# A graph attention layer: the mish ratio in the products' PSUM bank, and gathers that wait for the products 14 groups back

## The chip, the core and the metric

One core of a Trainium2 chip runs the kernel. The metric is the device time of one execution in microseconds (us); shorter is better. The engines are TensorE (PE, its weight loads PEld), VectorE (DVE), ScalarE (ACT), GpSimd (POOL) and SyncE (SP, which issues most of the plain DMAs). Each runs its own instructions strictly in order; semaphores tie them together.

## What is computed

A graph of 6250 nodes (128 features, 4 heads of 32) and 206250 edges, sorted by receiver. The reference, cut to what matters:

```python
e_att  = nodes[senders] @ Ws + Ws_b + edges @ We + We_b      # per edge, 4 heads x 32
recv   = nodes[receivers] @ Wr + Wr_b
logits = einsum(mish(e_att + recv), attn_w) + attn_b         # mish(x) = x * tanh(softplus(x))
w      = exp(logits - segment_max(logits, receivers))
w      = w / segment_sum(w, receivers)[receivers]
x      = layernorm(x + segment_sum(w * e_att, receivers))
```

## The kernel before

**Tables first.** A prologue computes two tables, `xs_table` (nodes times Ws, with biases) and `xr_table` (nodes times Wr), on PE (L754) and DVE (L1042), and stores them to HBM.

**Windows and groups.** The edges are then worked off in 51 windows of 4096 edges (128 partitions by 32 columns). A window has 8 groups (`NG`) of 4 columns, numbered g = 0 to 7; there are 408 groups. With `at(w, g) = w * 8 + g + 1` the groups are counted through, and every semaphore of a per-group step is compared with such a count.

**One group** goes through these steps, each one instruction on 128x512 numbers unless a count is given:

- POOL gathers the 4 columns of sender rows, `gathers`, L717, 4 indirect DMAs, into the buffer `gath` in SBUF (named `landing` in the profile). Two windows fit, so a buffer is used again 16 groups later.
- DVE makes the one-hot matrices of the receivers, `one_hots`, L1113. PE transposes edges and one-hots, `turn`, L793 and L798; ACT copies both out of PSUM, L907 and L914.
- PE multiplies, `products`, L815 and L816, 16 matrix instructions, into one of two banks, `ps_z[g % 2]`.
- DVE adds the gathered rows, `add_gathered`, L1122, from `ps_z` into `Z` in SBUF; its semaphore is `z_ready`.
- ACT computes the mish ratio in `tbuf` (SBUF) in five instructions, L923 to L939; the last one gives `ratio_ready`.
- DVE forms mish (L1129, semaphore `mish_ready`), the scores (L1138) and their sums per head (L1144).
- A window later, when the maxima of the segments are known, DVE scales `Z` (`messages`, L1205) and PE sums it per receiver (`sums`, L827, 8 matrix instructions per group).

**The order is written by hand.** Each engine has a function `window` that goes through g = 0 to 7 (below, "step g" of an engine). What a step holds:

- PE, step g: `products(g)`, `turn` of the group two ahead, then old sums: in steps 0 to 3 the groups 4 to 7 of two windows ago, in steps 5, 6, 7 the groups 0, then 1, then 2 and 3 of the window before.
- ACT, step g: the two copies of the group two ahead, then the five ratio instructions of group g.
- DVE, step g: `one_hots` of the group three ahead, `add_gathered(g)`, messages (none in step 3, two in step 4, else one), then `mish`, `score` and `reduce_heads` of group g - 1. Small instructions of the softmax and the layer norm (`aside`) stand between them in steps 3 to 6.

The one-hot buffer holds two windows, so `one_hots` waits until the sum of the group 16 earlier has been taken (`sum_ready`). In DVE's steps 5, 6 and 7 that sum stands at the end of PE's step of the same number; in steps 0 to 4 it stands in PE's step before. `products(g)` waits for the copies of its own group and for the add of group g - 2, which read its bank. POOL's gathers of a group wait for the products `AHEAD` groups back.

Of the kernel before, what the change touches and what calls it, by code (L numbers as in the profile page):

```python
# [21 lines left out]
ACT = mybir.ActivationFunctionType  # L22
# [3 lines left out]
D = 128  # L26
# [11 lines left out]
TINY = 1e-30  # L38
EPS = 1e-5
PREP = 6  # L40
AHEAD = 4
SEG_A, SEG_B, SEG_C = 3, 3, 5
ENDS_READ = 2
SEG = SEG_A + SEG_B + SEG_C
# [23 lines left out]
def gat_kernel(nc, x, src, dst, edges, ws_k, ws_b, wr_k, wr_b, we_k, we_b, attn_w, attn_b, out):  # L68
# [14 lines left out]
    with ctx:  # L83
        def sb(name, shape, dt=F32):
            return ctx.enter_context(nc.sbuf_tensor(name, shape, dt))

        def sem(name):
            return ctx.enter_context(nc.semaphore(name))
# [14 lines left out]
        Zv = Z[:, :, :].rearrange("p b (t c) -> p b t c", c=ZC)  # L103
# [52 lines left out]
        c_ln2 = sb("c_ln2", [P, 1])  # L156
# [32 lines left out]
        def ps(name, shape):  # L189
            return ctx.enter_context(nc.psum_tensor(name, shape, F32))  # L190
# [3 lines left out]
        ps_z = [ps(f"ps_z{i}", [P, GT, D]) for i in range(2)]  # L194
# [68 lines left out]
        z_ready = sem("z_ready")  # L263
# [4 lines left out]
        ratio_ready = sem("ratio_ready")  # L268
        mish_ready = sem("mish_ready")
# [17 lines left out]
        def at(w, g):  # L287

            return w * NG + g + 1

        def wait(eng, s, value):

            if not isinstance(value, int) or value > 0:
                eng.wait_ge(s, value)

        def wait_apart(eng, s, value, past):


            eng.wait_ge(s, value)
            eng.sem_inc(past, 1)  # L300

        def there(w):

            return not isinstance(w, int) or 0 <= w < W
# [398 lines left out]
        def _(pool):  # L703
# [7 lines left out]
            def gathers(w, b):  # L711

                for g, (a, n) in enumerate(GROUPS):
                    if not isinstance(w, int) or at(w, g) > AHEAD:
                        wait_apart(pool, z_ps, at(w, g) - AHEAD, past_pool)
                    for t in range(a, a + n):
# [22 lines left out]
        def _(pe):  # L739
# [62 lines left out]
            def products(w, b, k, g):  # L802

                a, n = GROUPS[g]
                q = g % 2
                pe.wait_ge(edgeT_ready, at(w, g))
                pe.wait_ge(onehotT_ready, at(w, g))
                wait(pe, z_ready, at(w, g) - 2)
                if g == 0:
                    if not there(w - 1):  # L810
                        pe.wait_ge(s_first_xr, 1)
                    else:
                        pe.wait_ge(xr_landed[b], k * 16 + (16 if b else 0))
                for j in range(n):
                    nc.tensor.matmul(ps_z[q][:, j, :], edgeT[:, q, j, :], we_sb[:, :], start=True, stop=False)  # L815
                    mm = nc.tensor.matmul(ps_z[q][:, j, :], onehotT[:, q, j, :], xr_buf[:, b, :],  # L816
                                          start=False, stop=True)
                mm.then_inc(z_ps, 1)
# [56 lines left out]
        def _(act):  # L875
# [50 lines left out]
            def ratio_step(w, g, k):  # L926
                tb = tbuf[:, g % NT, 0:GROUPS[g][1] * D]
                if k == 0:
                    act.wait_ge(bounded, at(w, g))
                    nc.scalar.activation(tb, tb, ACT.Exp, bias=c_zmax[:, 0:1], scale=-1.0).then_inc(exp_done, 1)  # L930
                elif k == 1:
                    act.wait_ge(exp_done, at(w, g))
                    nc.scalar.activation(tb, tb, ACT.Square, bias=c_one[:, 0:1]).then_inc(sq_done, 1)  # L933
                elif k == 2:
                    act.wait_ge(sq_done, at(w, g))
                    nc.scalar.activation(tb, tb, ACT.Ln, bias=c_one[:, 0:1]).then_inc(ln_done, 1)  # L936
                else:
                    act.wait_ge(ln_done, at(w, g))
                    nc.scalar.activation(tb, tb, ACT.Exp, bias=c_ln2[:, 0:1], scale=-1.0).then_inc(ratio_ready, 1)  # L939

            def items(w):
                act.wait_ge(ends_ps, w + 1)
# [47 lines left out]
        def _(dve):  # L990
# [45 lines left out]
            for done in range(2 * NB):  # L1036
                a, n = BATCHES[done % NB]
                stage, bias = (xs_stage, bias_s) if done < NB else (xr_stage, bias_r)
# [86 lines left out]
            def mish(w, b, g):  # L1125
                a, n = GROUPS[g]
                dve.wait_ge(ratio_ready, at(w, g))
                tb = tbuf[:, g % NT, 0:n * D].rearrange("p (t d) -> p t d", d=D)
                nc.vector.scalar_tensor_tensor(out=tb, in0=tb, scalar=1.0, in1=Zv[:, b, a:a + n, 0:D],  # L1129
                                               op0=ALU.subtract, op1=ALU.mult, reverse0=True)\  # L1130
                    .then_inc(mish_ready, 1)

# [214 lines left out]
```

## Time and profile before

| | |
|---|---|
| Three runs | 2601.63, 2613.3, 2615.81 us; median 2613.3 us |
| Profiled execution, from its first to its last instruction (span) | 2661.8 us |
| Busy: PE, DVE, ACT, POOL | 1917.4, 1895.0, 1927.7, 1575.1 us |
| Mean granted TensorE clock | 0.835 of full speed |
| Bytes over HBM | 240.18 MB, 90 GB/s on average |

The span of the profiled execution is 48.5 us (1.9%) above the median of the runs, though it leaves out what lies before its first and after its last instruction. No separate time of that execution is listed beside its span. Busy times are averages over steps with different limits: an engine at 72% can be the one that all wait for in one step and idle in the next. "remote" in a row means that the wait ended by a semaphore update that the profile does not pin to an instruction that ended just before it; "issue" means that no wait is seen.

### The profile page before, as it was taken

The page shows a single profiled execution, that of the slowest core. Times are in us where ns is not written, and L with a number is a line of the kernel's source. Part 1 is how long each engine was busy: PE and PEld are TensorE (multiplying, and loading weights), DVE is VectorE, ACT ScalarE, POOL GpSimd, SP SyncE. Part 2 cuts the span into 40 slices and gives each one's busy share as a digit, 9 for nine tenths or more (in the row PEclk, how much of TensorE's full clock was granted, in tenths as well). Part 3 has the DMA queues.
Part 4 walks back from the last instruction along what each step waited for, and adds up shares of the span by engine and source line. Part 5 has one row for each costly group of instructions (what it writes and reads, how often), then busy time and mean ns, then how long its engine had stood idle before and what let it go on. Part 6 is the DMA issues. An engine that isn't in the chain of part 4 may idle for free.

```text
span 2661.8 us, 45397 instructions
## 1 busy us (share of the span) xinstructions
PE 1917.4 (72%) x13621; PEld 1789.2 (67%) x13621; DVE 1895.0 (71%) x3941; ACT 1927.7 (72%) x3126; POOL 1575.1 (59%) x1640
## 2 busy tenths in 40 slices
PE   5667777777776777776776777776777777776776
PEld 5567666766666776766666766666667676666665
DVE  2676777777777767776676777766777777677766
ACT  1777777777777777777777777777777777777774
POOL 2666656656666665666566656656666666556661
PEclk8888888888888887888888888878888888878877
DMA  6422322322232322232232232232223232223220
GB/s 191 130 77 80 105 83 78 112 79 77 81 111 77 97 96 77 77 113 79 76 112 79 78 105 86 78 100 90 78 93 99 79 98 95 77 86 104 79 79 17
DMA packets 106714, 240.18 MB, mean 90 GB/s; under 512 B 45800, under 2 KB 72546, under 8 KB 99658
## 3 DMA queue, kind: packets, MB, share of 16 engines
q1 hardware_dynamic: 53334, 132.54, 14.6%
q0 software_dynamic: 52224, 107.06, 14.1%
q10 hardware_dynamic: 1128, 0.25, 0.0%
q8 instruction: 13, 0.21, 0.0%
q14 instruction: 15, 0.12, 0.0%
HBM read 229.98 MB, written 9.74 MB: 90 GB/s over the span
## 4 chain that ended last, share of the span: by engine, by line
DVE 36%; PE 20%; another core or an unknown queue 18%; issue 17%; ACT 7%; DVEq 1%; DMA 1%; ACTq 0%; SPq 0%
PE ps_sum L827 7%; DVE Z L1122 6%; DVE tbuf L1138 6%; DVE tbuf L1129 6%; DVE Z L1205 5%; PE ps_z L815 4%; PE ps_z L816 4%; DVE onehot L1113 4%; DVE logit L1144 2%; PE ps_edgeT L793 2%; ACT tbuf L933 1%; ACT tbuf L930 1%; ACT tbuf L936 1%; ACT tbuf L923 1%
## 5 line engine op out<-in xcount | busy, mean ns | idle before, releaser
L717 POOL DMA_INDIRECT landing<-xs_table,src_i x1632 | 1574.2, 965 | 1034.1 <-issue 448.3
L815 PE MATMUL ps_z<-we_sb,edgeT 128*128 128x128 f32 x3264 | 767.2, 320 | 83.3 <-issue 82.4
L816 PE MATMUL ps_z<-xr_buf,onehotT 128*128 128x128 f32 x3264 | 751.9, 315 | 72.3 <-issue 71.5
L827 PE MATMUL ps_sum<-Z,onehot 128*128 128x132 f32 x3264 | 558.9, 321 | 204.7 <-DVE att L1224 95.2
L815 PEld LDWEIGHTS ps_z<-we_sb,edgeT 128*128 128x128 f32 x3264 | 613.0, 232 | 100.9 <-issue 97.3
L816 PEld LDWEIGHTS ps_z<-xr_buf,onehotT 128*128 128x128 f32 x3264 | 609.4, 231 | 83.1 <-issue 82.8
L827 PEld LDWEIGHTS ps_sum<-Z,onehot 128*128 128x128 f32 x3264 | 485.6, 224 | 223.8 <-issue 149.4
L1113 DVE TENSOR_TENSOR onehot<-iota_f,ps_dve 128x512 f32<-128x512 f32 x408 | 276.0, 677 | 432.5 <-remote 352.6
L923 ACT ACTIVATE tbuf<-Z,c_zmax 128x512 f32<-128x512 f32 x408 | 296.2, 726 | 165.7 <-DVE Z L1122 85.9
L907 ACT COPY edgeT<-ps_edgeT 128x512 f32<-128x512 f32 x408 | 235.3, 577 | 229.4 <-remote 179.9
L798 PE MATMUL ps_onehotT<-ident_half,onehot 128*128 128x128 bf16 x1632 | 176.6, 232 | 241.8 <-issue 103.8
L1122 DVE TENSOR_TENSOR Z<-ps_z,landing 128x512 f32<-128x512 f32 x408 | 278.5, 683 | 88.6 <-remote 72.9
L914 ACT CAST onehotT<-ps_onehotT 128x512 f32<-128x512 bf16 x408 | 238.8, 585 | 132.9 <-remote 120.5
L798 PEld LDWEIGHTS ps_onehotT<-ident_half,onehot 128*128 128x128 bf16 x1632 | 125.0, 104 | 291.3 <-issue 226.7
L930 ACT ACTIVATE tbuf<-tbuf,c_zmax 128x512 f32<-128x512 f32 x408 | 294.7, 722 | 13.3
L793 PE MATMUL ps_edgeT<-ident,landing 128*128 128x128 f32 x1632 | 281.1, 295 | 32.3 <-issue 31.9
L933 ACT ACTIVATE tbuf<-tbuf,c_one 128x512 f32<-128x512 f32 x408 | 294.6, 722 | 13.3
L936 ACT ACTIVATE tbuf<-tbuf,c_one 128x512 f32<-128x512 f32 x408 | 294.5, 722 | 13.3
L939 ACT ACTIVATE tbuf<-tbuf,c_ln 128x512 f32<-128x512 f32 x408 | 294.0, 721 | 11.6
L1129 DVE SCALAR_TENSOR_TENSOR tbuf<-tbuf,Z 128x512 f32<-128x512 f32 x408 | 279.3, 685 | 26.6 <-ACT tbuf L939 21.2
L1138 DVE TENSOR_TENSOR tbuf<-tbuf,ps_dve 128x512 f32<-128x512 f32 x408 | 278.4, 682 | 9.0
L1144 DVE TENSOR_REDUCE logit<-tbuf 128x16 f32<-128x512 f32 x408 | 277.9, 681 | 7.3
(110 smaller groups left out, 1228.3 us busy)
## 6 DMA issues: line engine op xcount, KB each, us to landing
landing<-in_edge_attr_dram SPq DMA_DIRECT2D x51, 2048.0 KB
landing<-xs_table,src_i POOLq DMA_INDIRECT x1632
x_in<-in_x_dram SPq DMA_DIRECT2D x51, 64.0 KB
xr_in<-xr_table SPq DMA_DIRECT2D x51, 64.0 KB
out_dram<-y_out SPq DMA_DIRECT2D x51, 64.0 KB
xr_buf<-xr_table SPq DMA_DIRECT2D x50, 64.0 KB
xs_table<-onehot SPq DMA_DIRECT2D x2, 896.0 KB
xr_table<-landing SPq DMA_DIRECT2D x1, 1568.0 KB
```

The source lines that it names most:

```text
L717: nc.gpsimd.indirect_dma_start(gath[b][:, t, :], None, xs_dram, bass.IndirectOffsetOnAxis(ap=src_i[:, b, t:t + 1], axis=0))\
L793: tr = nc.tensor.transpose(ps_edgeT[g % 2][:, j, :], edge_buf[:, b, a + j, :], ident[:, :])
L815: nc.tensor.matmul(ps_z[q][:, j, :], edgeT[:, q, j, :], we_sb[:, :], start=True, stop=False)
L816: mm = nc.tensor.matmul(ps_z[q][:, j, :], onehotT[:, q, j, :], xr_buf[:, b, :], start=False, stop=True)
L827: mm = nc.tensor.matmul(ps_sum[:, 0:ZC], OHv[:, b, t, :], Zv[:, b, t, :], start=(t == 0), stop=(t == T - 1))
L923: nc.scalar.activation(tb, Zv[:, b, a:a + n, 0:D], ACT.Relu, bias=c_zmax[:, 0:1], scale=-1.0)\
L930: nc.scalar.activation(tb, tb, ACT.Exp, bias=c_zmax[:, 0:1], scale=-1.0).then_inc(exp_done, 1)
L1113: nc.vector.tensor_tensor(OHv[:, b, a:a + n, :], iota_f[:, :].unsqueeze(1).to_broadcast([P, n, P]), local[:, b, a:a + n].unsqueeze(2).to_b ...
L1122: nc.vector.tensor_tensor(Zv[:, b, a:a + n, 0:D], ps_z[g % 2][:, 0:n, :], gath[b][:, a:a + n, :], ALU.add).then_inc(z_ready, 1)
L1129: nc.vector.scalar_tensor_tensor(out=tb, in0=tb, scalar=1.0, in1=Zv[:, b, a:a + n, 0:D], op0=ALU.subtract, op1=ALU.mult, reverse0=True)\
L1138: nc.vector.tensor_tensor(tb, tb, row.to_broadcast([P, n, D]), ALU.mult).then_inc(scored, 1)
L1144: nc.vector.tensor_reduce(logit[:, b, :, a:a + n].rearrange("p h t -> p t h"), tb, AX.X, ALU.add)\
```

## The change

Three things change. ACT's last ratio instruction writes to the bank `ps_z[g % 2]`, which the group's own products had filled and the add has read, instead of to `tbuf`. DVE's mish instruction takes the ratio from there, so it reads one operand from PSUM and one from SBUF instead of two from SBUF; its output is still `tbuf`. Since the bank is now in use for longer, `products(g)` waits for `mish` of group g - 2 instead of for its add. Apart from that, `AHEAD` goes from 4 to 14. A group's products wait for mish, hence for the add, of two groups earlier, so products 14 back still imply the add 16 back that has freed the gather buffer.

```diff
-AHEAD = 4
+AHEAD = 14
...
                 pe.wait_ge(edgeT_ready, at(w, g))
                 pe.wait_ge(onehotT_ready, at(w, g))
-                wait(pe, z_ready, at(w, g) - 2)
+                wait(pe, mish_ready, at(w, g) - 2)
...
                     act.wait_ge(ln_done, at(w, g))
-                    nc.scalar.activation(tb, tb, ACT.Exp, bias=c_ln2[:, 0:1], scale=-1.0).then_inc(ratio_ready, 1)
+                    nc.scalar.activation(ps_z[g % 2][:, :, :].rearrange("p t d -> p (t d)"), tb, ACT.Exp,
+                                         bias=c_ln2[:, 0:1], scale=-1.0).then_inc(ratio_ready, 1)
...
                 dve.wait_ge(ratio_ready, at(w, g))
                 tb = tbuf[:, g % NT, 0:n * D].rearrange("p (t d) -> p t d", d=D)
-                nc.vector.scalar_tensor_tensor(out=tb, in0=tb, scalar=1.0, in1=Zv[:, b, a:a + n, 0:D],
+                nc.vector.scalar_tensor_tensor(out=tb, in0=ps_z[g % 2][:, :, :], scalar=1.0, in1=Zv[:, b, a:a + n, 0:D],
                                                op0=ALU.subtract, op1=ALU.mult, reverse0=True)\
                     .then_inc(mish_ready, 1)
```

No instruction of PE, DVE or ACT changes its place; on POOL waits fall away ahead of the first groups. On PE the place that matters is a step of the window loop: the wait of the products now names `mish_ready`, and behind it, in the same in-order queue, stand the transposes of the group two ahead and a sum. After the change a piece of the loop reads:

```order
L815 MATMUL ps_z<-we_sb,edgeT 128x128 [waits mish_ready,onehotT_ready,edgeT_ready]
L816 MATMUL ps_z<-xr_buf,onehotT 128x128
L815 MATMUL ps_z<-we_sb,edgeT 128x128
L816 MATMUL ps_z<-xr_buf,onehotT 128x128
L815 MATMUL ps_z<-we_sb,edgeT 128x128
L816 MATMUL ps_z<-xr_buf,onehotT 128x128
L815 MATMUL ps_z<-we_sb,edgeT 128x128
L816 MATMUL ps_z<-xr_buf,onehotT 128x128
L793 MATMUL ps_edgeT<-ident,landing 128x128 [waits edgeT_ready]
L793 MATMUL ps_edgeT<-ident,landing 128x128 x3
L798 MATMUL ps_onehotT<-ident_half,onehot 128x128 [waits onehotT_ready,onehot_ready]
L798 MATMUL ps_onehotT<-ident_half,onehot 128x128 x3
```

Before, the first of these rows named `z_ready` in that place; the rest is the same.

On POOL the place is the start of the program: the gathers of windows 0 and 1 in the order in which they are issued (`landing` is the gather buffer, `z_ps` the semaphore of the products). A piece of the difference, before with -, after with +:

```order
 L717 DMA landing<-xs_table,src_i 128x128 [waits src_landed0,s_table]
-L717 DMA landing<-xs_table,src_i 128x128 x15
-L717 DMA landing<-xs_table,src_i 128x128 [waits z_ps]
-L717 DMA landing<-xs_table,src_i 128x128 x3
-L717 DMA landing<-xs_table,src_i 128x128 [waits z_ps]
-L717 DMA landing<-xs_table,src_i 128x128 x3
...
+L717 DMA landing<-xs_table,src_i 128x128 x31
+L717 DMA landing<-xs_table,src_i 128x128 [waits src_landed1,s_xrtable,s_search]
+L717 DMA landing<-xs_table,src_i 128x128 x23
```

Before, POOL stopped after 16 gathers and then after every 4; now it issues the 32 gathers of window 0 without a stop, and 24 of window 1 after that.

## Rows read from the trace of the kernel before

**Rows 1.** The page, part 1: busy time and share of each engine

```profile
PE 1917.4 (72%) x13621; PEld 1789.2 (67%) x13621; DVE 1895.0 (71%) x3941; ACT 1927.7 (72%) x3126; POOL 1575.1 (59%) x1640
```

**Rows 2.** Waits: engine, instruction, waited-for, us in total, times, longest

```profile
POOL landing L717 <- remote: 364.1, 147, 3.4
DVE onehot L1113 <- remote: 352.6, 104, 9.5
...
DVE onehot L1113 <- PE ps_sum L827: 53.7, 43, 5.6
```

**Rows 3.** Timeline 974 to 991 us: PE, DVE, POOL (start, duration; idle before in brackets)

```profile
979.56 1.12 PE L827 MATMUL ps_sum<-Z,onehot 128*128 128x132 f32 x8
...
989.75 0.64 PE L815 MATMUL ps_z<-we_sb,edgeT 128*128 128x128 f32 x2
...
987.68 0.69 DVE L1113 TENSOR_TENSOR onehot<-iota_f,ps_dve 128x512 f32<-128x512 f32 x1 [3.77 <-remote]
...
989.48 0.68 DVE L1129 SCALAR_TENSOR_TENSOR tbuf<-tbuf,Z 128x512 f32<-128x512 f32 x1
...
984.90 0.94 POOL L717 DMA_INDIRECT landing<-xs_table,src_i  x1 [0.30 <-issue]
988.64 0.94 POOL L717 DMA_INDIRECT landing<-xs_table,src_i  x1 [2.79 <-remote]
```

**Rows 4.** Timeline of DVE, 1005 to 1020 us: steps 4 to 7 of one window

```profile
1005.86 0.68 DVE L1129 SCALAR_TENSOR_TENSOR tbuf<-tbuf,Z 128x512 f32<-128x512 f32 x1
...
1009.99 0.69 DVE L1113 TENSOR_TENSOR onehot<-iota_f,ps_dve 128x512 f32<-128x512 f32 x1 [1.39 <-PE ps_sum L827]
...
1011.99 0.68 DVE L1129 SCALAR_TENSOR_TENSOR tbuf<-tbuf,Z 128x512 f32<-128x512 f32 x1
...
1015.01 0.69 DVE L1113 TENSOR_TENSOR onehot<-iota_f,ps_dve 128x512 f32<-128x512 f32 x1 [0.67 <-PE ps_sum L827]
...
1016.82 0.68 DVE L1129 SCALAR_TENSOR_TENSOR tbuf<-tbuf,Z 128x512 f32<-128x512 f32 x1
...
1019.49 0.69 DVE L1113 TENSOR_TENSOR onehot<-iota_f,ps_dve 128x512 f32<-128x512 f32 x1
```

**Rows 5.** Timeline of PE in the same stretch: products and sums

```profile
1007.74 2.12 PE L827 MATMUL ps_sum<-Z,onehot 128*128 128x132 f32 x8 [2.76 <-DVE att L1224]
1009.65 0.64 PE L815 MATMUL ps_z<-we_sb,edgeT 128*128 128x128 f32 x2
...
1013.86 1.12 PE L827 MATMUL ps_sum<-Z,onehot 128*128 128x132 f32 x8
1014.81 0.38 PE L815 MATMUL ps_z<-we_sb,edgeT 128*128 128x128 f32 x2
...
1017.26 2.02 PE L827 MATMUL ps_sum<-Z,onehot 128*128 128x132 f32 x16
```

**Rows 6.** Timeline of POOL in the same stretch: one gather

```profile
1017.17 1.14 POOL L717 DMA_INDIRECT landing<-xs_table,src_i  x1 [0.30 <-issue]
```

**Rows 7.** Groups of instructions: busy us, mean ns of one, idle before

```profile
L717 POOL DMA_INDIRECT landing<-xs_table,src_i x1632 | 1574.2, 965 | 1034.1 <-issue 448.3 <-remote 364.1 <-PE ps_z L816 185.0
...
L939 ACT ACTIVATE tbuf<-tbuf,c_ln 128x512 f32<-128x512 f32 x408 | 294.0, 721 | 11.6
...
L1129 DVE SCALAR_TENSOR_TENSOR tbuf<-tbuf,Z 128x512 f32<-128x512 f32 x408 | 279.3, 685 | 26.6 <-ACT tbuf L939 21.2 <-issue 5.0
L1122 DVE TENSOR_TENSOR Z<-ps_z,landing 128x512 f32<-128x512 f32 x408 | 278.5, 683 | 88.6 <-remote 72.9 <-PE ps_z L816 14.1 <-issue 1.3
...
L907 ACT COPY edgeT<-ps_edgeT 128x512 f32<-128x512 f32 x408 | 235.3, 577 | 229.4 <-remote 179.9 <-PE ps_edgeT L793 45.7 <-issue 3.4
```

**Rows 8.** Timeline of DVE, then of POOL, in the prologue

```profile
56.85 0.69 DVE L1042 TENSOR_TENSOR landing<-ps_z,bias_r 125x512 f32<-125x512 f32 x1 [5.67 <-remote]
...
66.51 0.42 DVE L1042 TENSOR_TENSOR landing<-ps_z,bias_r 125x256 f32<-125x256 f32 x1 [0.16 <-PE ps_z L754]
...
73.63 0.94 POOL L717 DMA_INDIRECT landing<-xs_table,src_i  x1 [15.45 <-PE ps_z L816]
```

## The prediction, made before the changed kernel ran

> **What bounds the kernel now.** I read the page first. It shows no engine that is the limit: PE, DVE and ACT are each busy for 71 to 72% of the span [rows 1]. Divided by 408 groups, ACT needs 4.7 us a group and the span has 6.5. So the time is in waits, and the second view is the list of waits. Its longest rows are two of one kind [rows 2]: POOL waits 364 us, 147 times, and DVE's one-hots wait 353 us, 104 times, both for something called "remote".
>
> The third view, the timeline, tells what that is [rows 3]. PE's sum ended by the record at 979.56 + 1.12 = 980.68, but the one-hots that wait for it started at 987.68, after 3.77 us of idle time. POOL's run of gathers ended at 984.90 + 0.94 = 985.84, DVE went on 1.8 us later and POOL 2.8 us later. The prologue shows the same: while POOL gathers without a stop, the adds L1042 that wait for PE stand 5.67 us apart from the work before them; the last of them, well after the run has ended, waits 0.16 us [rows 8]. I read it so: a finished piece of PE's work becomes known late once POOL has gathered back to back for some microseconds, and everything held becomes known 1 to 2 us after POOL pauses. I call that a hold. The trace does not say what the mechanism is. It gives the kernel a rhythm: POOL gets two products, issues eight gathers at 1.25 us each (0.94 and a gap of 0.30), then pauses some 2.5 us; 12.4 us for two groups.
>
> The gathers themselves are not late. The adds' idle time is 88.6 us in all, 72.9 of it "remote", 14.1 behind the products, and no row names a gather [rows 7].
>
> Last, the undisturbed steps. In DVE's steps 5, 6 and 7 the one-hots wait for the sum at the end of PE's step of the same number: the waits of 1.39 and 0.67 us behind "PE ps_sum" [rows 4]. There PE paces DVE directly.
>
> **The new wait.** In DVE's step g, mish of group g - 1 stands behind the one-hots, the add and the messages; products(g + 1) now wait for it. Behind those products, in PE's queue, stand the transposes and the sum, and for the sum waits DVE's next step. So in steps 5 to 7 two stretches that ran side by side run one after the other: DVE from the one-hots to the end of mish, then PE from the products to the end of the sum.
>
> Step 5 to 6: DVE's one-hots start at 1009.99, mish ends at 1011.99 + 0.68 = 1012.67, 2.68 us [rows 4]. PE from products to the end of the sum takes 1009.65 to 1013.86 + 1.12 = 1014.98, 5.33 us [rows 5]. One after the other: 1009.99 + 2.68 + 5.33 = 1018.0, where the next one-hots now start at 1015.01. Plus 3.0 us. PE was at the slower of its two clocks there.
>
> Step 6 to 7: one-hots 1015.01, mish ends 1017.50, 2.49 us. PE, now at the faster clock, goes from 1014.81 to the middle of its double sum, 1017.26 + 1.01 = 1018.27: 3.46 us. Together 1020.96 against 1019.49, plus 1.5 us.
>
> Step 4 to 5: mish ended at 1005.86 + 0.68 = 1006.54. Products of 1.8 us (fast) to 3.4 us (slow) and transposes of 0.7 us would put the sum at 1009.0 to 1010.7, where it started at 1007.74 behind DVE's att [rows 4, 5]. Plus 1.3 to 3.0; I take 1.5, nearer the fast clock, at which PE spends most of its time (the mean granted clock is 0.835 of full speed).
>
> Steps 7 to 3: DVE does not wait for the sum of the same step. There products, add, messages and mish form a ring of 1.8 + 0.6 + 0.6 + 0.7 plus small change, about 4.0 us at the fast clock and 5.5 at the slow one, beside ACT's 4.7. Undisturbed that is hidden. After a hold it is not quite: DVE's mish ended at 989.48 + 0.68 = 990.16, and products had started at 989.75 [rows 3], 0.4 us earlier; where PE had worked a whole group ahead during the hold, up to 1.3 us. Four holds a window, at 0.25 us each: plus 1.0 us.
>
> Sum: 3.0 + 1.5 + 1.5 + 1.0 = 7.0 us a window, times 51 windows: 357 us.
>
> **The longer lead.** In the steady state POOL is the faster party (5.0 us a group against 6.2), so with a lead of 4 or of 14 it catches up and then waits for each product: the same pace and about the same runs. Since no add waits for a gather, the lead gains nothing. It costs at the start. Now POOL pauses from 58.2 to 73.63, 15.45 us [rows 8], and five of the adds L1042 get through between 56.85 and 66.51 in 9.7 us. After the change POOL goes on for another 16 gathers of 1.25 us, from 58.2 to 78.2; these adds come out of the hold at about 80 instead of 66.5. Plus 13 us, and up to 10 more for the next unbroken run of 24 gathers; I take 15. It is not below zero, because nothing on that path waits for a gather. The queue of SP loads the senders of a window some 17 groups before POOL needs them at its new lead; that is just early enough, so I put no price on it.
>
> **Mish with one SBUF operand.** A gather that starts beside mish takes longer: 1.14 us at 1017.17 instead of 0.94, beside the mish of 1016.82 [rows 4, 6]. The mean is 965 ns; the excess over 940 is 25 ns times 1632, 41 us of POOL's time at most [rows 7]. The Trainium skill (SBUF — State Buffer, Who interferes with whom) says that a DVE instruction with two SBUF inputs contends with a GpSimd instruction that reads SBUF; by that rule the change takes the contention away, and this row agrees. POOL is no longer what others wait for, so I count a quarter: minus 10 us, bounds 0 and 41.
>
> Does the PSUM operand itself cost DVE time? The add, with one operand in PSUM, takes 683 ns, mish with both in SBUF 685 [rows 7]: I count nothing. The Trainium skill (VectorE: DVE Perf Modes, on the TRN2 errata) gives a PSUM source 62 cycles more than an SBUF source at 0.96 GHz; as an estimate from that page, 65 ns times 408 would add 26 us. The trace disagrees, and the measurement decides.
>
> ACT's write to PSUM: no row shows ACT writing there. The nearest are 721 ns (SBUF to SBUF) and 577 ns (PSUM to SBUF) [rows 7]: 0 to 144 ns a group, 0 to 59 us if all were on the path. The ratio is ready before mish wants it in steps 5 to 7 (no wait stands at either mish [rows 4]), so I take zero.
>
> **The sum** against the profiled span: 2661.8 + 357 + 15 - 10 = 3024. The runs' median is 0.982 of that span, so the 362 us become 355, and the runs 2613.3 + 355 = 2968 us. Its own range: 3 us a window (only the steps 5 to 7 at the fast clock, 1.5 and 1.5) with all gains taken, 2613 + 150 + 15 - 41 - 20, about 2720 as the extreme, 2800 more likely; 9 us a window (slow clock in every step) and 25 at the start, 2613 + 451 + 25, about 3090.
>
> **Rivals.** *The holds go, and it gets faster.* If a lead of 14 spreads the gathers into runs of four with a pause after each, PE's work is never held. The waits called "remote" on the one-hots and adds are 353 + 73 us [rows 2, 7]; were all of them to go, and the new ring to cost only its fast-clock part of 4 us a window (204 us), and 41 and 0 to 59 us to come off, the time would be 2613 - 426 + 204 - 60, about 2330 at best; with half of the waits gone about 2545. It decides if more than 7 us a window of holds vanish. For it speaks that the adds of the prologue run freely once POOL pauses [rows 8]; against it, that POOL's rate does not change and a catch-up run needs only two products close together. Chance 0.09, time 2540.
>
> *The wait is met anyway.* If mish(g - 2) were always done when products(g) could start, only the small terms stay: 2613 + 15 - 10, about 2615. Against it stand 1009.65 for the products and 1012.67 for the mish they would need [rows 4, 5]. Chance 0.05.
>
> *Longer runs, longer holds.* With 14 groups of freedom POOL does not pause when PE is late, say after a late load of senders; runs of 12 to 16 gathers then hold PE for 6 us and more (the longest wait of the one-hots is 9.5 [rows 2]), and now the ring passes through PE and DVE twice as often. At two more holds of 2.5 us a window: 2968 + 250, about 3200. Chance 0.12.
>
> *My forecast*: 0.74, of which a few in a hundred end below 2720.
>
> **How the numbers follow.** The likeliest case gives 2968. Below 2800 lie the two rivals at or under 2615 (0.14) and little of the forecast's own; above 3100 lies most of the third rival. The range 2780 to 3100 leaves out some 0.2. This kernel's runs differ by up to 0.5%, so 0.5% is about what can be told from no change. Faster 0.10, same 0.03, slower 0.87.
>
> **What the new profile would show.** Waits "PE ps_z <- DVE tbuf" (mish) of some 2.5 us at the products in steps 5 to 7, 100 to 150 or more in all; the distance of the one-hots in those steps near 6 to 8 us; PE, DVE and ACT busy for nearer 64%; gathers at 940 ns; the last L1042 near 80 us. Wrong would be: one-hots of steps 5 to 7 still 5 us apart, or waits called "remote" that fall below 150 us.

## The result, and the profile after

The changed kernel took 2838.2 us (median of four runs, 2803.9 to 2843.4) and the kernel before 2614.6 us (four runs, 2601.6 to 2620.9). The ratio is 1.084, 95% interval 1.077 to 1.091: slower by 224 us. I had predicted 2968 us. (A ratio, here and below, leaves out executions more than 1.5% above the fastest one of the same kernel; there was one such, in the kernel with the wait alone and a lead of 14.)

The page of the kernel after, parts 1 and 4 (busy time by engine, then the chain that ended last), and three groups of its part 5:

```profile
PE 1830.8 (65%) x13621; PEld 1730.2 (61%) x13621; DVE 1898.6 (67%) x3941; ACT 1943.4 (69%) x3126; POOL 1553.1 (55%) x1640
...
PE 38%; DVE 32%; issue 14%; another core or an unknown queue 10%; ACT 5%; DVEq 1%; DMA 1%; SPq 0%; ACTq 0%
...
L717 POOL DMA_INDIRECT landing<-xs_table,src_i x1632 | 1552.1, 951 | 1169.9 <-issue 472.1
...
L939 ACT ACTIVATE ps_z<-tbuf,c_ln 128x512 f32<-128x512 f32 x408 | 281.2, 689 | 11.6
...
L1130 DVE SCALAR_TENSOR_TENSOR tbuf<-ps_z,Z 128x512 f32<-128x512 f32 x408 | 278.1, 682 | 5.8 <-ACT ps_z L939 5.8
```

DVE's work is the same as in [rows 1], its share fell from 71% to 67%: the time went into waits. (I had written nearer 64% for PE, DVE and ACT; it is 65, 67 and 69%.) (Lines from L940 on have moved by one; mish is now L1130.) Mish takes 682 ns with an operand from PSUM, 685 before [rows 7]. ACT's last instruction takes 689 ns where it took 721: writing to PSUM is 32 ns shorter. A gather takes 951 ns, not 965.

The waits of the kernel after (engine, instruction, waited for: us in total, times, longest):

```profile
PE ps_z L815 <- DVE tbuf L1130: 687.9, 291, 7.5
...
POOL landing L717 <- PE ps_z L816: 455.7, 198, 8.2
DVE onehot L1114 <- PE ps_sum L827: 432.6, 143, 5.1
...
POOL landing L717 <- remote: 179.4, 88, 7.9
ACT edgeT L907 <- remote: 172.7, 99, 32.3
```

The first row did not exist before: PE's products wait 688 us for mish. By the trace they start 0.15 us after mish of two groups earlier ends (medians by step, windows 2 to 49; 0.19 us in step 0); before, they had started 1.6 to 6.3 us ahead of that end. Second, the one-hots' wait behind the sum grew from 54 to 433 us [rows 2]. Third, what I had called holds shrank: waits with "remote" add up over all engines to 1237 us before and 700 us after. Fourth, the mean granted TensorE clock rose from 0.835 to 0.874 of full speed, which I had not forecast. In the middle of the program, over some eight windows each, PE was busy for 294 us at 0.83 before (1000 to 1402 us) and for 277 us at 0.89 after (1000 to 1422 us).

DVE between two one-hots, in the middle of the program (start, duration, idle before in brackets), and PE's products in the same stretch:

```profile
1212.44 0.69 DVE L1114 TENSOR_TENSOR onehot<-iota_f,ps_dve 128x512 f32<-128x512 f32 x1 [3.67 <-PE ps_sum L827]
1213.04 0.68 DVE L1123 TENSOR_TENSOR Z<-ps_z,landing 128x512 f32<-128x512 f32 x1
...
1214.44 0.68 DVE L1130 SCALAR_TENSOR_TENSOR tbuf<-ps_z,Z 128x512 f32<-128x512 f32 x1
...
1220.39 0.69 DVE L1114 TENSOR_TENSOR onehot<-iota_f,ps_dve 128x512 f32<-128x512 f32 x1 [3.60 <-PE ps_sum L827]
```

```profile
1215.26 0.76 PE L815 MATMUL ps_z<-we_sb,edgeT 128*128 128x128 f32 x2 [2.96 <-DVE tbuf L1130]
```

This is the serial line: one-hots at 1212.44, mish ends at 1215.12, products start at 1215.26, then transposes and the sum, then the next one-hots at 1220.39. One step is 7.95 us; the same step of a window in [rows 4] was 5.02.

At the start of the program, DVE, then POOL, then ACT:

```profile
84.77 0.42 DVE L1043 TENSOR_TENSOR landing<-ps_z,bias_r 125x256 f32<-125x256 f32 x1 [0.71 <-PE ps_z L754]
...
137.48 0.69 DVE L1123 TENSOR_TENSOR Z<-ps_z,landing 128x512 f32<-128x512 f32 x1 [27.22 <-remote]
...
162.82 0.69 DVE L1123 TENSOR_TENSOR Z<-ps_z,landing 128x512 f32<-128x512 f32 x1 [21.73 <-remote]
```

```profile
100.81 0.94 POOL L717 DMA_INDIRECT landing<-xs_table,src_i  x1 [23.24 <-DMA src_i<-in_src_dram]
...
154.68 0.94 POOL L717 DMA_INDIRECT landing<-xs_table,src_i  x1 [0.30 <-issue]
163.57 0.94 POOL L717 DMA_INDIRECT landing<-xs_table,src_i  x1 [7.95 <-remote]
```

```profile
149.38 0.59 ACT L907 COPY edgeT<-ps_edgeT 128x512 f32<-128x512 f32 x1 [32.28 <-remote]
```

After the run of window 0, POOL waited for the senders of window 1 and then issued 44 gathers without a pause, 100.81 to 155.6. From 110 to 163 us two adds waited 27.2 and 21.7 us. The first of them went on at 137.48, and ACT's copy at 149.38, both in the middle of that run: what is held does not always wait for a pause of POOL, as I had read it. The add of group 16 stands at 232.0 us, where it stood at 172.1: the start got 60 us longer. From there to the last add it is 2564.6 us against 2452.3.

### The profile page after: what moved, and what is told of

It reads as the page before. It is cut to its first block, busy times and chain, and to the rows that moved or that the text cites. A ratio compares the mean times of both kernels' runs of the same rounds, so it can differ in the third digit from the quotient of the medians.

```text
span 2832.6 us, 45435 instructions
## 1 busy us (share of the span) xinstructions
PE 1830.8 (65%) x13621; PEld 1730.2 (61%) x13621; DVE 1898.6 (67%) x3941; ACT 1943.4 (69%) x3126; POOL 1553.1 (55%) x1640
## 4 chain that ended last, share of the span: by engine, by line
PE 38%; DVE 32%; issue 14%; another core or an unknown queue 10%; ACT 5%; DVEq 1%; DMA 1%; SPq 0%; ACTq 0%
PE ps_z L815 14%; PE ps_z L816 12%; DVE tbuf L1130 7%; DVE Z L1123 7%; PE ps_sum L827 6%; DVE Z L1206 6%; PE ps_edgeT L793 3%; DVE tbuf L1139 3%; DVE onehot L1114 2%; PE ps_onehotT L798 2%; DVE logit L1145 1%; ACT tbuf L930 1%; ACT tbuf L936 1%; ACT tbuf L933 1%
## 5 line engine op out<-in xcount | busy, mean ns | idle before, releaser
L717 POOL DMA_INDIRECT landing<-xs_table,src_i x1632 | 1552.1, 951 | 1169.9 <-issue 472.1
L815 PE MATMUL ps_z<-we_sb,edgeT 128*128 128x128 f32 x3264 | 782.2, 328 | 873.7 <-DVE tbuf L1130 687.9
L815 PEld LDWEIGHTS ps_z<-we_sb,edgeT 128*128 128x128 f32 x3264 | 600.9, 229 | 940.9 <-issue 887.2
L827 PE MATMUL ps_sum<-Z,onehot 128*128 128x132 f32 x3264 | 470.7, 291 | 24.6 <-issue 18.1
L827 PEld LDWEIGHTS ps_sum<-Z,onehot 128*128 128x128 f32 x3264 | 418.9, 199 | 30.6 <-issue 23.9
L936 ACT ACTIVATE tbuf<-tbuf,c_one 128x512 f32<-128x512 f32 x408 | 294.6, 722 | 13.3
L933 ACT ACTIVATE tbuf<-tbuf,c_one 128x512 f32<-128x512 f32 x408 | 294.6, 722 | 13.3
L930 ACT ACTIVATE tbuf<-tbuf,c_zmax 128x512 f32<-128x512 f32 x408 | 294.6, 722 | 13.3
L939 ACT ACTIVATE ps_z<-tbuf,c_ln 128x512 f32<-128x512 f32 x408 | 281.2, 689 | 11.6
L1130 DVE SCALAR_TENSOR_TENSOR tbuf<-ps_z,Z 128x512 f32<-128x512 f32 x408 | 278.1, 682 | 5.8 <-ACT ps_z L939 5.8
L1206 DVE TENSOR_TENSOR Z<-Z,ps_dve 128x512 f32<-128x512 f32 x408 | 272.2, 678 | 1.8
L793 PEld LDWEIGHTS ps_edgeT<-ident,landing 128*128 128x128 f32 x1632 | 224.2, 159 | 2.9 <-issue 2.8
```

What stands on the lines that cost most here:

```text
L717: nc.gpsimd.indirect_dma_start(gath[b][:, t, :], None, xs_dram, bass.IndirectOffsetOnAxis(ap=src_i[:, b, t:t + 1], axis=0))\
L793: tr = nc.tensor.transpose(ps_edgeT[g % 2][:, j, :], edge_buf[:, b, a + j, :], ident[:, :])
L827: mm = nc.tensor.matmul(ps_sum[:, 0:ZC], OHv[:, b, t, :], Zv[:, b, t, :], start=(t == 0), stop=(t == T - 1))
L1130: nc.vector.scalar_tensor_tensor(out=tb, in0=ps_z[g % 2][:, :, :], scalar=1.0, in1=Zv[:, b, a:a + n, 0:D], op0=ALU.subtract, op1=ALU.mult, ...
L1206: nc.vector.tensor_tensor(zz, zz, ww, ALU.mult).then_inc(msg_ready, 1)
```

## The experiments

The kernels below ran on three chips, on which the unchanged kernel before takes 2174 us, not 2615. On which chip the pair above ran is not on record; I call it the first chip, but whether it is a fourth one, or one of these three in another condition, is not shown. Kernels are compared only with the kernel before on the same chip. The two with the lead alone or the old lead, the wait alone and the late lead form one group (before: 2173.7 us); the unchanged kernels, the plain DMAs and mish ahead of the add another (2173.6); the three with mish at the head and the wait with the lead of 14 a third (2176.7). The expectations of the first group were written before I knew how much faster these chips run the kernel, so their times in us do not apply.

### The unchanged kernels on such a chip

Both files as they are.

> The kernel before, unchanged, for a profile on the chip on which the other kernels of this call run. In the call before this one it took 2174 us instead of 2615, and the kernels run beside it showed no hold at all. Theory: whether PE's finished work is held while POOL gathers is a property of the chip or of its state, not of the program; so this run is either near 2615 us with waits called remote of some 900 us, or near 2174 us with none and POOL gathering without a pause. Rival: the holds come and go from run to run on one chip; then its runs spread over hundreds of us.

> The changed kernel, unchanged, on this chip. Theory: without holds the wait for mish costs 4.5 to 5.8 us a window (the two kernels with that wait showed windows of 45.5 and 46.8 us against 41.0) and the lead costs nothing: about 2455 us, ratio 1.13. With holds: 2838 us, ratio 1.08, 60 us of it at the start. Rival: the lead of 14 costs at the start without holds too: then 2500 us or more beside a kernel before of 2174 us.

Measured: before 2171.6 us, ratio 0.999 [0.998, 1.000]; after 2464.2 us, ratio 1.133 [1.131, 1.135]. No wait in either trace carries the word "remote", nor in any other of these twelve. Waits and gathers of the kernel before here:

```profile
POOL landing L717 <- issue: 476.9, 1564, 0.7
...
DVE Z L1122 <- DMA landing<-xs_table,src_i: 144.2, 58, 4.3
```

```profile
POOL 37%; issue 20%; ACT 15%; PE 11%; DMA 8%; DVE 8%; POOLq 1%; ACTq 0%; DVEq 0%; SPq 0%
...
L717 POOL DMA_INDIRECT landing<-xs_table,src_i x1632 | 1594.8, 977 | 533.2 <-issue 476.9
```

Without holds the kernel before is bound by POOL: it gathers from beginning to end without a pause over 0.7 us, 1632 times 0.977 plus a gap of 0.30, and the adds wait for gathers. The kernel after:

```profile
PE ps_z L815 <- DVE tbuf L1130: 672.8, 358, 3.1
DVE onehot L1114 <- PE ps_sum L827: 456.2, 146, 5.1
...
POOL landing L717 <- PE ps_z L816: 250.6, 156, 4.3
```

Now POOL waits for products, and the serial line is the bound. The traces give the mean time from one add to the next, by group of the window (worked out from the starts of DVE's adds, windows 2 to 49):

| us, step g to g + 1 | 0 | 1 | 2 | 3 | 4 | 5 | 6 | 7 |
|---|---|---|---|---|---|---|---|---|
| before, first chip | 5.93 | 5.55 | 6.60 | 7.16 | 7.54 | 5.83 | 6.98 | 4.79 |
| after, first chip | 6.18 | 5.33 | 6.94 | 6.25 | 9.08 | 7.45 | 6.95 | 4.56 |
| before, other chip | 6.86 | 5.33 | 5.59 | 3.99 | 6.47 | 4.27 | 4.30 | 4.11 |
| after, other chip | 5.08 | 4.09 | 5.59 | 3.98 | 8.81 | 7.64 | 7.49 | 4.26 |
| mish at the head, steps 4 to 7 (see below), third chip | 5.18 | 4.22 | 5.85 | 6.01 | 5.66 | 5.66 | 5.67 | 3.37 |

On the chip without holds the change adds 2.3, 3.4 and 3.2 us in steps 4, 5 and 6, and gets 3.0 back in steps 0 and 1, where the kernel before waited for gathers: 6.0 us a window, times 51 windows 306 us, against a measured difference of 291. A lower clock is not behind it: the mean granted clock in the two traces is 0.919 before and 0.917 after. On the first chip most of the extra time stands in steps 4 and 5, 1.5 and 1.6 us; step 6 is unchanged and step 3 is 0.9 us shorter.

### One part of the change at a time

The lead alone, in the kernel before (first); the kernel after with the old lead (second):

```diff
-AHEAD = 4
+AHEAD = 14
```

```diff
-AHEAD = 14
+AHEAD = 4
```

> The kernel before with the lead of POOL's gathers alone raised from 4 to 14; ratio in SBUF, products wait for the add two groups back. My theory: the lead costs only at the start, where POOL now issues 32 and then 44 gathers without a pause and PE's finished work is held meanwhile. The changed kernel's add of group 16 came 60 us later than before's, so some 45 to 60 us: 2660 to 2675 us; windows after the second as before, about 50 us. Rival A, my first sum (13 to 25 us at the start): 2630 us. Rival B, the lead spreads the runs and takes holds away in the steady state: below 2600 us.

> The changed kernel with the lead back at 4: ratio in PSUM and the wait for mish alone. My theory: all of the change's cost behind the start is this wait, some 3.3 us a window, 165 us: about 2780 us (2750 to 2800), and the first windows end as early as before's. Rival, the lead of 14 shares in the cost of the later windows or takes some of it off: this kernel is then more than 30 us away from 2780.

Measured: the lead alone 2172.3 us, ratio 1.000 [0.999, 1.001]; the kernel after with the old lead 2463.6 us, 1.133 [1.130, 1.136], the same as the whole change. The lead is worth nothing here, either way.

The wait alone, ratio left in SBUF, lead 4:

```diff
-                wait(pe, z_ready, at(w, g) - 2)
+                wait(pe, mish_ready, at(w, g) - 2)
```

> The kernel before (ratio in SBUF, lead 4) with only the wait of the products changed from the add to mish of two groups back. My theory: the wait alone makes the cost, and the ratio's place in PSUM gives 0 to 20 us back (gathers at 951 instead of 965 ns, ACT's last step 689 instead of 721 ns): 2780 to 2810 us. Rival, the PSUM place itself costs or gains more: more than 40 us from the kernel with the ratio in PSUM and the same lead.

Measured: 2404.2 us, 1.107 [1.104, 1.109]. Its two longest waits of this kind:

```profile
PE ps_z L815 <- DVE tbuf L1129: 671.5, 355, 3.0
...
DVE onehot L1113 <- PE ps_sum L827: 390.5, 147, 5.4
```

So one changed name in a wait makes 230 us of the 290. The other 60 looked like the price of the ratio's place in PSUM, and are more than the 40 us that I had set for that rival. The same wait with the lead of 14 tested that:

```diff
-AHEAD = 4
+AHEAD = 14
...
-                wait(pe, z_ready, at(w, g) - 2)
+                wait(pe, mish_ready, at(w, g) - 2)
```

> The kernel before with the products' wait for mish and gathers 14 groups ahead, the ratio left in SBUF. The wait alone with 4 ahead took 2404 us; the whole change took 2464 us, and with 4 ahead 2464 us too. Theory A (the 60 us between them come with the ratio's place in PSUM, the lead is worth nothing): 2395 to 2410 us. Theory B (they come from how TensorE's granted clock falls in one schedule or the other, which the lead moves too): anything else, most likely 2420 to 2465 us, with more of the span at the slow clock than the 10% that the wait alone showed between 500 and 1900 us.

Measured: 1.106 [1.103, 1.110] from the first four of the five executions listed here, whose median of 2408 us is what theory A says. But the five executions of this one kernel were 2404.6, 2404.9, 2411.9, 2416.7 and 2470.9 us, at mean granted clocks of 0.940, 0.940, 0.938, 0.936 and 0.914. The kernels with the ratio in PSUM (lead 4 and lead 14) had 2459 to 2469 us at 0.913 to 0.917, the wait with lead 4 had 2402 to 2407 at 0.940 to 0.943. All lie near one line of time against clock, some 66 us for 0.026 of clock. One stretch of the wait with lead 4, then of the wait with lead 14 in the execution of 2470.9 us (busy time by engine, then granted clock, DMA share, GB/s):

```profile
500.00:1000.00 500.00, 350.19 (x2882) 332.37 (x2882) 402.13 (x835) 412.12 (x670) 350.89 (x352) 0.95 0.32 99
```

```profile
500.00:1000.00 500.00, 353.69 (x2794) 336.19 (x2793) 389.62 (x805) 398.70 (x649) 344.50 (x351) 0.92 0.32 98
```

In the same 500 us the second gets 3% fewer matrix instructions done. So one execution reached the longer time without the PSUM operand, and at the same clock as the kernels that have it. That speaks for theory B: the 60 us go with how much of the products' work gets the slower clock, and not with the time of the PSUM operand itself. In the trace at 0.914, about half of the products of groups 5, 6 and 7 run at the slower clock (over 2.6 us for a group instead of 2.0); in the other a third of those of group 6 and two thirds of group 7. It rests on one execution of nine with the wait for mish and the ratio in SBUF. The eight others took 2402 to 2417 us, and all eight with the ratio in PSUM 2459 to 2469. Why the place of the ratio goes with the slower clock stays open.

### The lead late

The kernel after, with lead 4 in windows 0 and 1 and 14 from then on.

```diff
+                    ahead = 4 if isinstance(w, int) and w < 2 else AHEAD
-                    if not isinstance(w, int) or at(w, g) > AHEAD:
-                        wait_apart(pool, z_ps, at(w, g) - AHEAD, past_pool)
+                    if not isinstance(w, int) or at(w, g) > ahead:
+                        wait_apart(pool, z_ps, at(w, g) - ahead, past_pool)
```

> The changed kernel, but the gathers of windows 0 and 1 wait for the products 4 back and only those of the loop 14 back. My theory: the start's cost of some 60 us goes, the rest stays: about 2780 us, equal to the changed kernel with a lead of 4. Rival, POOL makes up the ten groups of lead in one long run when the loop begins, and the hold is only moved: then 2820 to 2840 us, with a wait of over 15 us in window 2.

Measured: 2452.2 us, 1.127 [1.124, 1.130]; its executions, 2442 to 2462 us at clocks of 0.925 to 0.917, lie on the same line. This was meant to take away the 60 us that the start cost on the first chip. Without holds there is no such loss to take away, so it says nothing on that.

### Plain DMAs in place of the gathers

The kernel before, in which each gather is a plain DMA of the first 128 rows of the table: the sender rows are left out of the computation.

```diff
-                        nc.gpsimd.indirect_dma_start(
-                            gath[b][:, t, :], None, xs_dram,
-                            bass.IndirectOffsetOnAxis(ap=src_i[:, b, t:t + 1], axis=0))\
+                        nc.gpsimd.dma_start(gath[b][:, t, :], xs_dram[0:P, :])\
```

> The kernel before, with each indirect gather of POOL replaced by a plain DMA from the same queue that brings the first 128 rows of the table; so the sender rows are left out and the result is not the reference's. Bytes, queue, semaphores and waits stay. Theory: a hold needs POOL to work out gather descriptors back to back; with plain DMAs there is none, on either kind of chip, and the time falls to what ACT and DVE need, 2050 to 2150 us. Rival: the holds come with the DMA traffic or with the semaphore updates of the gathers: on a chip with holds the time stays above 2400 us.

Measured: 2067.4 us, 0.951 [0.949, 0.953].

```profile
ACT 66%; issue 16%; DVE 9%; PE 7%; ACTq 1%; DMA 1%; DVEq 0%; SPq 0%
...
L717 POOL DMA_DIRECT2D landing<-xs_table x1632 | 861.7, 535 | 1147.0 <-PE ps_z L814 1061.6
```

With an issue of 535 ns instead of 977, POOL waits for the products and ACT is the bound. That confirms what bounds the kernel before on this chip. It was meant to test whether indirect DMAs make the holds; as there are none here, that was not tested.

### Mish earlier in DVE's step

If the cost is the line from one-hots over add, messages and mish to the products, mish should be moved towards the front of it. First the kernel after with mish ahead of the add, in all eight steps:

```diff
                         one_hots(w1, b1, g1)
+                    if there(w0):
+                        mish(w0, b0, g0)
                     if there(w):
                         add_gathered(w, b, k, g)
...
-                    if there(w0):
-                        mish(w0, b0, g0)
```

> The changed kernel, with mish of group g - 1 put ahead of the add of group g in DVE's step instead of behind the add and the messages. Theory: what costs is that products(g + 1), and the sum and the one-hots behind them, stand in line behind one-hots, add, messages and mish. With mish 1.2 us earlier in each step, the steps 4, 5 and 6 get 1.2 us shorter each: 3.6 us a window, 180 us: 2275 us without holds, 2660 with. Rival: mish has to wait for ACT's ratio where it now stands (it had 0.2 to 4.4 us to spare in the kernels with the new wait), the add gets later, and ACT and DVE lose as much as PE gains: no gain over 50 us, or a loss.

Measured: 2304.0 us, 1.060 [1.058, 1.061]. More than half of the loss is gone, 160 us where I had expected 180, with every part of the change still in. The granted clock rose too, from 0.913 to 0.917 in the changed kernel to 0.943 to 0.949 here. By the line of time against clock above, an estimate, a rise of 0.03 can go with some 75 of the 160 us; the shorter line and the clock were not separated. Then mish ahead of the one-hots too, in the steps of groups 4 to 7 only, and with it two variants: one that also has mish right behind the add in the steps of groups 0 to 3, and the kernel before with the edit below and nothing else.

```diff
+                    if g >= 4 and there(w0):
+                        mish(w0, b0, g0)
                     if there(w1) and there(w):
                         one_hots(w1, b1, g1)
...
-                    if there(w0):
+                    if g < 4 and there(w0):
                         mish(w0, b0, g0)
```

> The changed kernel, with mish of the group before put at the very head of VectorE's step, ahead of the one-hots and the add, in the steps of groups 4 to 7 of each window; in groups 0 to 3 it stands where it was. Theory (the cost is the serial line add, ratio, mish, products in steps 4 to 6, since mish stands behind the add and the messages): in those steps the products now wait for little, the median wait of the products for mish falls from 3.1 us to under 1 us and its sum from 673 us to under 150 us, a window falls from 46.9 us to 41 us or below, and GpSimd's gathers are the bound again, at 951 ns instead of 977 ns because mish no longer reads two SBUF operands: 1632 x (0.951 + 0.30) + 85 = about 2130 us, range 2110 to 2210, where the kernel before takes 2174 us. Rival (the ratio is late, mish only waits at another place and holds the one-hots and the add behind it): VectorE waits for ScalarE's ratio in each of these steps, over 1 us each, and the time is 2280 to 2350 us. If this chip shows the long holds of TensorE's signals beside the gathers (the kernel before at about 2615 us), the theory says a ratio below 1.03 and the rival one above 1.05.

> The same, and in groups 0 to 3 of each window mish stands right behind the add instead of behind the messages. Theory: in groups 0 to 3 mish was not waited for long (the slack from ratio to mish was 0.25 to 2.0 us there), so this adds nothing: within 0.5% of the kernel with mish at the head in groups 4 to 7 alone. Rival: the add and messages of groups 0 to 3 are delayed by 0.7 us each and a window grows by 1 to 2 us: 2.5 to 4% above it.

> The kernel before (ratio in SBUF, no wait of the products for mish, gathers 4 groups ahead) with mish at the head of the step in groups 4 to 7: the order alone. Theory: the kernel before is bound by the gathers' issue on GpSimd here, 1632 x (0.977 + 0.30) = 2084 us and about 85 us of start and end, and the order of VectorE doesn't touch that: 2160 to 2190 us, a ratio of 0.995 to 1.005. Rival: the order is a gain by itself, 2130 us or below, in which case what the changed kernel with mish at the head gains is none of the change's.

Measured, in this order: 2212.7 us, 1.016 [1.014, 1.018]; 2217.7 us, 1.019 [1.016, 1.021]; 2226.5 us, 1.023 [1.020, 1.025]. Neither of my two expectations for the first held: it is above the 2130 us of my theory (range 2110 to 2210) and below the 2280 to 2350 us of the rival, and the products' wait is 385 us where I had said below 150. Its waits, then DVE, then the products of PE, then ACT:

```profile
PE ps_z L815 <- DVE tbuf L1130: 385.3, 300, 3.1
DVE tbuf L1130 <- ACT ps_z L939: 222.7, 193, 2.5
```

```profile
1004.76 0.69 DVE L1130 SCALAR_TENSOR_TENSOR tbuf<-ps_z,Z 128x512 f32<-128x512 f32 x1 [1.18 <-ACT ps_z L939]
1005.37 0.68 DVE L1114 TENSOR_TENSOR onehot<-iota_f,ps_dve 128x512 f32<-128x512 f32 x1
1005.96 0.68 DVE L1123 TENSOR_TENSOR Z<-ps_z,landing 128x512 f32<-128x512 f32 x1
...
1010.42 0.69 DVE L1130 SCALAR_TENSOR_TENSOR tbuf<-ps_z,Z 128x512 f32<-128x512 f32 x1 [1.43 <-ACT ps_z L939]
1011.03 0.68 DVE L1114 TENSOR_TENSOR onehot<-iota_f,ps_dve 128x512 f32<-128x512 f32 x1
1011.63 0.68 DVE L1123 TENSOR_TENSOR Z<-ps_z,landing 128x512 f32<-128x512 f32 x1
```

```profile
1005.60 0.46 PE L815 MATMUL ps_z<-we_sb,edgeT 128*128 128x128 f32 x2 [2.03 <-DVE tbuf L1130]
...
1007.90 0.63 PE L816 MATMUL ps_z<-xr_buf,onehotT 128*128 128x128 f32 x2
```

```profile
1006.68 0.72 ACT L923 ACTIVATE tbuf<-Z,c_zmax 128x512 f32<-128x512 f32 x1 [0.96 <-DVE Z L1123]
...
1009.70 0.69 ACT L939 ACTIVATE ps_z<-tbuf,c_ln 128x512 f32<-128x512 f32 x1
```

The products still wait 2.03 us for mish, but they end at 1008.5, 3.1 us ahead of the add at 1011.63 that needs them: that wait is now covered. What closes the step is another line, through DVE and ACT: add at 1005.96, five ACT instructions to 1010.39, mish at 1010.42, one-hots, add at 1011.63. That is 5.67 us, step after step, in the steps of groups 4 to 6 (last row of the table). The kernel before with the same order has steps of 6.0, 5.7 and 5.7 us there, so this line is the order's price, not the change's; I had expected 0.995 to 1.005 for that kernel, not 1.023. The second variant, with mish right behind the add in the steps of groups 0 to 3, differs by 5 us (0.2%), within the 0.5% of my theory.

Between the first and the last of the three the order is the same and only the change differs: 2209.9 to 2213.3 us in five executions against 2224.0 to 2229.9, a ratio of the medians of 0.994. Where the wait is covered, the three parts of the change together are a gain of 0.6%. The granted clock differs as well, 0.954 to 0.956 with the change and 0.911 to 0.914 without, so how much of that gain is the clock's is not known. Neither order beats the kernel before on this chip.

## Why the prediction was right, and where it was not

**The new wait: right.** The line "from the one-hots to the end of mish, then PE from the products to the end of the sum" is what the traces show, where I put it: in steps 4 to 6 of the table without holds, in steps 4 and 5 on the first chip. That it is the cause is shown on the chips without holds: the name in the wait alone gives 1.107, and an order that shortens the line takes most of the loss away with the wait still there. My 100 to 150 us "or more" for the waits of the products was far too low against 688; most of these waits cost nothing by themselves, since the products are only late if the add or the sum wants them earlier. The size per window was 7.0 us by my sum (3.0 + 1.5 + 1.5 + 1.0). The chip without holds shows 8.9, less the 3.0 that steps 0 and 1 gave back: for step 4 to 5 2.3 us where I had 1.5, for 5 to 6 3.4 where I had 3.0, for 6 to 7 3.2 where I had 1.5, and nothing for steps 7 to 3, where I had 1.0.

**On the first chip a window grew by 2.4 us, not 7.0** (50.4 to 52.7, sums of the first two rows of the table). Part of that gap is the profiled execution of before, which was 1.9% above the runs: against their median (50.4 times 0.982 is 49.5) it is about 3.3 us, an estimate. The step of the prediction that failed is that POOL, with the longer lead, keeps "the same pace and about the same runs". POOL's runs of gathers, mostly of 8 before (149 runs of 8, 43 of 4, a run ending at a pause over 0.7 us), were mostly of 4 after (265 of 4, 38 of 8), and the waits called "remote" fell from 1237 to 700 us, those of the one-hots from 353 to 86. That is what the first rival described, at about half strength; I gave it 0.09 as a case of its own and left it out of the sum. By difference, 7.0 less 3.3, what the sum lacked is about minus 4 us a window. Fewer holds are not the only candidate for it: at the clock of 0.89 PE was busy for about 2 us less a window than at 0.83, and what of that lay on the path was not measured either. I had written that "remote" waits below 150 us would prove me wrong, and for the one-hots they were below. Whether the wait or the lead made POOL's runs shorter was not separated, as no experiment ran on a chip with holds. On the chip without them the changed kernel with the old lead of 4 has runs of 4 most often too (110 of them), where the kernel before has none, so there the wait is enough.

**The start: "I take 15", measured 60.** I gave the second unbroken run 24 gathers and at most 10 us. It was 44. POOL first stood 23.2 us waiting for the senders of window 1, which I had called loaded "just early enough" and priced at nothing. So it started at 100.81, 24 gathers went as forecast, and for each of the next 20 the product that it had to wait for (groups 0 to 4) was known when POOL came to it. The holds beside that run lasted 27 and 22 us. The trace of before had none longer than 9.5 [rows 2] to size them by, and by my own reading (a release 1 to 2 us after POOL pauses) a run of 44 times 1.25, 55 us, allowed for far more than 10. The last L1043 came at 84.8 us where I had said near 80.

**The small terms: right.** Mish with a PSUM operand costs nothing (682 against 685 ns). By the table of the Trainium skill (VectorE: DVE Perf Modes, on the TRN2 errata) each would have been some 65 ns longer, an estimate from its cycle counts; that does not show here. The gathers went to 951 ns, between 965 and the 940 that I named. On the other chips the step is 977 to 951, and the wait alone, with mish on two SBUF operands, has 997 against 951 for the same kernel with the ratio in PSUM: so it is the operand's place that does it. The Trainium skill (SBUF — State Buffer, Who interferes with whom) says that a DVE instruction with at most one SBUF input, outside its two-port modes, does not contend with GpSimd, and these rows agree. ACT's write to PSUM is 32 ns shorter; the Trainium skill (ScalarE: Activation LUTs, Step-by-step: what each stage is for) calls PSUM the faster destination, and this row agrees. What these terms gave in the whole time was not measured by itself.

**The errors offset each other in part.** The windows took 3.3 times 51, about 170 us, where I had 357; the start took 60 where I had 15. The one was too high by some 190, the other too low by 45, and the forecast was 130 us too high. There is some luck in that the time fell inside my range: with 15 us for the start it would have been near 2793, just above my lower bound of 2780, and that bound had no term for fewer holds or a higher clock. Of the other rivals, "the wait is met anyway" fell with the first row of the waits, and "longer runs, longer holds" was seen at the start of the program alone.

## What to carry to other kernels

A wait that names a later event of the same chain is to be priced by the loop it closes, step by step, from the engine that is waited for and back to it: here one name cost 10.7%, and moving the awaited instruction to the front of its step took the whole change from 13.3% down to 1.6%. When a wait has become long, look whether what stands behind it is needed; the version with mish at the head has such waits of 385 us in all and is no slower than the same order without them. And where a trace holds a loss of unknown cause, treat it as a term that the change can enlarge or shrink, and look whether the kernel shows it on another chip at all.

## What the runs showed of the hardware

- The same kernel took 2615 us for the pair above and 2172 to 2177 us on three chips. The 440 us come with waits that no instruction's end explains (1237 us over all engines, up to 32 us each in the kernel after), many of them beside unbroken runs of indirect gathers on POOL, and with a lower granted clock (0.835 against 0.919). On the three chips no trace has such a wait, though POOL gathers for 2090 us without a pause over 0.7 us on one of them (the unchanged kernel before). What differs stays open.
- One unchanged kernel got a granted TensorE clock of 0.940 on average in some executions and 0.914 in another, and took 2405 and 2471 us on the same chip (wait alone, lead 14).
- An indirect gather of 128 rows costs POOL 0.95 us and a gap of 0.30, or 0.965 to 0.997 on average where mish reads two SBUF operands; a plain DMA of the same size takes it 0.54 us.
